# A convolution, attention and mixture-of-experts block on one core: the output buffer's wait moved from the store one tile back to the store two tiles back

## The chip, the core and the metric

The kernel runs on one core of a Trainium2 chip. The metric is the device time of one execution in microseconds (us), the median of several runs. The engines are named as the profile names them: PE (matrix products), DVE (vector), ACT (activation functions), POOL (GpSimd, which here issues all indirect DMAs) and SP (which issues plain DMAs).

## What is computed

The input is `x` of shape (4, 256, 32, 32). A convolution block with attention comes first, then multi-head attention over 4 x 1024 tokens of 256 channels, and then a mixture of eight experts, each a two-layer network with 1024 hidden units, of which every token goes to its best two. This last stage is the one that the change touches.

```python
logits = flat @ Wr
top_vals, top_idx = jax.lax.top_k(logits, TOP_K)          # TOP_K = 2
top_w = jax.nn.softmax(top_vals, axis=-1)
gates = zeros((N, E)).at[jnp.arange(N)[:, None], top_idx].add(top_w)
for e in range(E):
    hdn = jax.nn.gelu(flat @ W1[e] + b1[e], approximate=False)
    y = hdn @ W2[e] + b2[e]
    out = out + gates[:, e:e + 1] * y
t = t + out
```

## The kernel before

The 8192 pairs of token and expert are sorted by expert into lists in DRAM. The expert stage runs over 40 tiles of them: 31 wide ones of 256 places (`PAIRS`) and 9 narrow ones of 128 (`SINGLES`). A last step reads the result back, transposes it and stores the output. Each engine runs its own stream in program order, and the streams meet at semaphores. The order is written out by hand. For tile t:

- SP loads the tile's list (`load_list`, line 570). It waits until the store of tile t-6 has landed. Lists from tile 8 on are also held until every scatter of the last batch has landed (line 587) and the last batch's normalised rows are stored (line 494, one transfer of 1 MB, which waits for the last `tail_low` of DVE, line 2204).
- POOL gathers the tile's rows by that list (`gather`, line 772). In POOL's loop, iteration t first issues the gather of tile t+3, then, in the first five iterations, two to four scatters of the last batch's list entries (line 742), then it waits for the store of tile t-1 to land and counts `y_out` up (`output_landed`, line 788), and then it waits for `y_kept` and issues the store of tile t (`store_output`, line 782). That store is an indirect DMA that adds into `res1_d` in DRAM, two of them for a wide tile. Stores are so never in flight for two tiles at once.
- PE, in iteration t: first products of tile t (`first`, line 1023), transpose of the gathered rows of tile t+1 (`turn`, line 1407, which waits for the gather), second products of tile t-1 (`second`, line 1448, which ends with `y_made`). The result lies in one of two halves of a PSUM bank.
- ACT computes the hidden units of tile t (`gelus`, line 993).
- DVE, in iteration t: splits the hidden units of tile t+1 in two parts (`split_hidden`, lines 2015 and 2017) and, within that, copies the transposed rows of tile t+2 for PE (`keep_turned`, line 2003) and, for narrow tiles, that tile's first weights (`copy_first`, line 2226). In iterations 0 to 4 it then does some steps for the lists and the last `tail_low` steps. Last comes `keep_output` of tile t (lines 2026 to 2036): it waits for `y_made` and for `y_out`, writes the output buffer `ysb[t % 2]`, multiplies it by the gates, and counts `y_kept` up.

There are two output buffers, `ysb[0]` and `ysb[1]`, used in turn. `FREE` is 1, the value from which these semaphores start. The last tile, 39, is not stored by POOL. It is placed by matrix products of PE (`place_last`, line 1023 after the tiles) once DVE has split it (`halves_of_last`, lines 2054 and 2056). SP reads the result back once the store of tile 38 has landed (lines 600 and 605), PE transposes it (line 1506), DVE adds the last tile (line 2064), and SP stores it.

Of the kernel before, what the change touches and what calls it, by code (L numbers as in the profile page):

```python
# [82 lines left out]
FREE = 1  # L83
# [31 lines left out]
def hybrid_block(nc, x, wk, bk, wv, bv, wq, bq, wwg, bn1_g, bn1_b, bn1_m, bn1_v, wout, bout,  # L115
# [3 lines left out]
    def sem(name):  # L119
        return ctx.enter_context(nc.semaphore(name))  # L120
# [15 lines left out]
    with ctx:  # L136
# [166 lines left out]
        LAST = TILES - 1  # L303
# [51 lines left out]
        def s(name):  # L355
            if name not in S:
                S[name] = sem(name)
            return S[name]
# [1154 lines left out]
        def _(dve):  # L1513
# [506 lines left out]
            def gates(slot, a):  # L2020

                return list_of(slot)[:, a, 2:3].bitcast(F32)

            def keep_output(t, u, e, slot, wide=True):
                n = 2 if wide else 1
                dve.wait_ge(s("y_made"), FREE + t + 1)
                dve.wait_ge(s("y_out"), FREE + t - (t == LAST))
                dve.scalar_tensor_tensor(  # L2028
                    out=ysb[u][:, 0:n], in0=PP[2][:, u * HALF:u * HALF + n * C].rearrange("p (a c) -> p a c", a=n),
                    scalar=1.0 / WSCALE, in1=b2b[:, bass.ds(e, 1), :].broadcast_to((P, n, C)),  # L2030
                    op0=ALU.mult, op1=ALU.add)
                dve.drain()
                for a in range(n):
                    op = dve.tensor_scalar(ysb[u][:, a], ysb[u][:, a], gates(slot, a), None, ALU.mult)  # L2034
                if t < LAST:
                    op.then_inc(s("y_kept"), 1)
# [199 lines left out]
            for t in range(TILES):  # L2236
# [24 lines left out]
                if t in MARK_AT:  # L2261
                    mark_tokens(MARK_AT.index(t))
                keep_output(t, t % 2, e, t, t < PAIRS)
                if t == 0:
                    dve.wait_ge(s("cnt_made"), 1)
# [33 lines left out]
```

## Time and profile before

| | us |
|---|---|
| runs of the kernel | 1181.81 median (1177.8, 1181.81, 1184.69) |
| span of the profiled execution | 1183.2 |
| busy in it: PE / DVE / ACT / POOL | 1105.0 / 818.8 / 628.7 / 600.2 |

The span runs from the first to the last instruction of the profiled execution. The page gives no other time of that execution. Its span lies 1.4 us above the median of the runs and within what they show, so a difference that is worked out in the span is carried over to the median as it is.

### The profile page before, as it was taken

How to read it: one execution, taken by the hardware profiler on the slowest of the kernel's cores; microseconds unless marked ns; L12 is line 12 of the kernel's file. 1: busy time of each engine (PE TensorE's matmuls, PEld its weight loads, DVE VectorE, ACT ScalarE, POOL GpSimd, SP SyncE). 2: the span in 40 equal slices, each digit the busy share in tenths (PEclk: the TensorE clock that was granted, in tenths of full speed). 3: DMA queues.
4: the chain of work that ended last, by engine and by line, in shares of the span. 5: the costliest groups of instructions: out<-in, count | busy, mean ns of one | idle time of the engine just before them, and what ended most of it. 6: DMA issues, size and time to landing. Idle time of an engine off the chain costs nothing.

```text
span 1183.2 us, 28483 instructions
## 1 busy us (share of the span) xinstructions
PE 1105.0 (93%) x10344; PEld 728.7 (62%) x10344; DVE 818.8 (69%) x1493; ACT 628.7 (53%) x1144; POOL 600.2 (51%) x513
## 2 busy tenths in 40 slices
PE   7999999978999999999999989898999999999995
PEld 4454645434444454555445545687899988989883
DVE  4666566766788788788878892768555656655773
ACT  3566676546677666766775665453333333333332
POOL 3424242314888763775477546167545445544540
PEclk9999999989999999999999999999999999999999
DMA  5356842626123230433243213723333233323328
GB/s 173 89 181 211 311 160 94 184 69 196 51 56 87 82 82 29 104 100 98 68 115 91 60 43 100 303 38 77 53 54 54 43 52 55 46 46 47 46 38 289
DMA packets 98884, 120.60 MB, mean 102 GB/s; under 512 B 29024, under 2 KB 76064, under 8 KB 98112
## 3 DMA queue, kind: packets, MB, share of 16 engines
q1 hardware_dynamic: 75280, 70.40, 20.3%
q0 software_dynamic: 20400, 42.08, 15.9%
q10 hardware_dynamic: 3072, 6.30, 1.5%
q8 instruction: 89, 1.46, 0.5%
q14 instruction: 43, 0.35, 0.1%
HBM read 73.10 MB, written 45.47 MB: 100 GB/s over the span
## 4 chain that ended last, share of the span: by engine, by line
PE 70%; DVE 11%; issue 6%; DMA 6%; ACT 3%; DVEq 3%; POOL 1%; SPq 1%; ACTq 0%; POOLq 0%
PE PP L1023 21%; PE PP L1448 11%; PE PP L1307 9%; PE PP L1333 8%; PE PP L1122 3%; DVE mxp L1739 3%; PE PP L1254 3%; PE PP L1194 3%; PE PP L1039 3%; PE PP L1322 2%; PE PP L1317 2%; DMA res_d<-WORK,lb 2%; PE PP L1154 1%; DVEq L2016 1%; DVE WORK L2017 1%
## 5 line engine op out<-in xcount | busy, mean ns | idle before, releaser
L953 ACT ACTIVATE WB<-PP 128x512 f32<-128x512 f32 x512 | 268.6, 606 | 146.1 <-PE PP L1333 146.0
L1739 DVE TENSOR_REDUCE mxp<-PP 128x2 f32<-128x1024 f32 x242 | 287.0, 1219 | 62.3 <-PE PP L1254 62.0
L993 ACT ACTIVATE WORK<-PP,b1c 128x256 f32<-128x256 f32 (+1 forms) x320 | 139.4, 450 | 239.4 <-PE PP L1023 191.7
L699 POOL TENSOR_TENSOR WB<-WB 128x1024 f32<-128x1024 f32 x84 | 197.8, 2358 | 89.4 <-PE PP L1322 58.7
L782 POOL DMA_INDIRECT res_d<-WORK,lb x70 | 117.6, 1680 | 157.8 <-DVE WORK L2034 144.7
L1448 PE MATMUL PP<-WB,WORK 128*128 x1704 | 193.8, 274 | 0.0
L1023 PE MATMUL PP<-WORK,WB 128*128 128x256 f16 (+1 forms) x1552 | 175.9, 273 | 2.4 <-DVE WORK L2003 1.7
L1448 PEld LDWEIGHTS PP<-WB,WORK 128*128 128x128 f16 x1704 | 165.2, 98 | 19.6
L1023 PE MATMUL PP<-WORK 128*128 128x128 f16 (+6 forms) x1086 | 161.1, 300 | 11.3 <-DVE WORK L1656 3.6
L1023 PEld LDWEIGHTS PP<-WORK,WB 128*128 (+1 forms) x1552 | 152.2, 102 | 22.2 <-issue 4.8
L1333 PE MATMUL PP<-WORK 97*128 97x256 f16 x1024 | 158.0, 277 | 6.7 <-ACT WB L953 4.2
L666 POOL TENSOR_TENSOR WB<-WORK,WB 128x1024 f16<-128x1024 f32 x32 | 68.8, 2151 | 168.4 <-ACT WORK L841 168.3
L1023 PEld LDWEIGHTS PP<-WORK 128*128 128x128 f16 (+1 forms) x1086 | 100.5, 118 | 73.2 <-issue 22.6
L1307 PE MATMUL PP<-WB,WORK 128*32 128x256 f32 x2048 | 139.4, 390 | 2.9 <-ACT WB L939 1.6
L1333 PEld LDWEIGHTS PP<-WORK 97*128 97x128 f16 x1024 | 84.1, 98 | 80.2 <-ACT WB L953 46.1
L2017 DVE TENSOR_TENSOR WORK<-WORK 128x512 f16<-128x512 f32 (+1 forms) x160 | 101.6, 635 | 13.0 <-issue 1.3
L742 POOL DMA_INDIRECT list_d<-meta,idx x64 | 62.6, 978 | 59.3 <-issue 15.6
L2028 DVE SCALAR_TENSOR_TENSOR WORK<-PP,WORK 128x512 f32<-128x512 f32 (+1 forms) x40 | 25.2, 631 | 97.0 <-PE PP L1448 84.2
L772 POOL DMA_INDIRECT WORK<-rows_d,lb x70 | 71.7, 1025 | 37.9 <-issue 35.5
L1307 PEld LDWEIGHTS PP<-WB,WORK 128*32 128x32 f32 x2048 | 56.1, 110 | 52.6 <-issue 31.7
L2015 DVE CAST WORK<-WORK 128x512 f16<-128x512 f32 (+1 forms) x160 | 65.3, 408 | 21.1 <-ACT WORK L993 16.6
L1254 PE MATMUL PP<-WB 32*128 32x512 f16 x484 | 48.4, 387 | 10.9 <-DVE mxp L1739 5.9
(319 smaller groups left out, 1205.1 us busy)
## 6 DMA issues: line engine op xcount, KB each, us to landing
WORK<-in_L_ffn_W_dram POOLq DMA_DIRECT2D x32, 512.0 KB, 4.3
res_d<-WORK SPq DMA_DIRECT2D x8, 1024.0 KB, 5.2
late_d<-WB POOLq DMA_DIRECT2D x1, 6144.0 KB, 19.3
WB<-late_d ACTq DMA_DIRECT2D x3, 2048.0 KB, 14.0
v_d<-WORK SPq DMA_DIRECT2D x4, 1024.0 KB, 5.2
WORK<-q_hi_d SPq DMA_DIRECT2D x16, 256.0 KB, 3.7
WORK<-v_d SPq DMA_DIRECT2D x8, 512.0 KB, 5.6
WORK<-k_hi_d SPq DMA_DIRECT2D x16, 256.0 KB, 3.9
```

The lines of the kernel that those rows point to most:

```text
L699: pool.tensor_tensor(PS[n % 2], PR[n % 3][:, 0], PR[n % 3][:, 1], ALU.add).then_inc(s("pair_kept"), 1)
L772: pool.indirect_dma_start(xs[t % 2][:, a].rearrange("p s c -> p (s c)"), None, rows_d[0:(B if t >= EARLY else B - 1) * N, :], bass.Indirec ...
L782: pool.indirect_dma_start(res1_d[:, :], bass.IndirectOffsetOnAxis(ap=lb[:, t % LISTS, a, 1:2], axis=0), ysb[u][:, a], None, compute_op=ALU ...
L953: act.activation(PR[n % 3][:, c // 2, c % 2 * 2:c % 2 * 2 + 2], SCORES[m % 3] .rearrange("p (h n) -> p h n", h=2), ACT.Exp).then_inc(s("e_ ...
L993: act.activation(hid[:, k, 0:width], hidden_bank(k)[:, 0:width], ACT.Gelu, bias=b1c[:, bass.ds(e, 1), k], scale=1.0 / WSCALE)\
L1023: mm = pe.matmul(dst, lhsT, rhs, start=(n == 0), stop=(n == len(pairs) - 1))
L1254: mm = pe.matmul(PP[2 + h // 2][:, h % 2 * HALF:(h % 2 + 1) * HALF], QM[rows_at, g, at:at + P], KM[rows_at, g, k * HALF:(k + 1) * HALF], s ...
L1307: pe.matmul(WEIGHED[h * D:(h + 1) * D, 0:QN], VV[par][:, 2 * s4 + i, h * D:(h + 1) * D], PR[n % 3][:, i, h], start=(s4 + i == 0), stop=(s4 ...
L1333: mm = pe.matmul(SCORES[m % 3][:, i * QN:(i + 1) * QN], KP[g][0:QK_ROWS + 1, h, j * P:(j + 1) * P], QP[0:QK_ROWS + 1, g, h, q:q + QN], sta ...
L1448: mm = pe.matmul(PP[2][:, u * HALF + a * C:u * HALF + (a + 1) * C], lhsT, rhs, start=(n == 0), stop=(n == len(pairs) - 1))
L1739: dve.tensor_reduce(mxp[:, n // 4 % 2, i, h:h + 2, k], PP[2 + h // 2][:, :].rearrange("p (h n) -> p h n", h=2), X_AXIS, ALU.max).then_inc( ...
L2017: dve.tensor_tensor(hs[u][:, 1, k, 0:width], hid[:, k, 0:width], hs[u][:, 0, k, 0:width], ALU.subtract).then_inc(s("hs_kept"), 1)
```

## The change

DVE's `keep_output` waits on `y_out` before it writes the buffer. Before, it waited until the store of tile t-1 had landed, except for the last tile, where it was the store of tile t-2. Now it is the store of tile t-2 for every tile, the one that read the same buffer; tile 0 doesn't wait. Nothing else differs.

```diff
             def keep_output(t, u, e, slot, wide=True):
                 n = 2 if wide else 1
                 dve.wait_ge(s("y_made"), FREE + t + 1)
-                dve.wait_ge(s("y_out"), FREE + t - (t == LAST))
+                if t:
+                    dve.wait_ge(s("y_out"), FREE + t - 1)
                 dve.scalar_tensor_tensor(
```

## Rows read from the trace of the kernel before

**Rows 1.** The page: the span and the busy time of PE.
```profile
span 1183.2 us, 28483 instructions
PE 1105.0 (93%) x10344; PEld 728.7 (62%) x10344; DVE 818.8 (69%) x1493; ACT 628.7 (53%) x1144; POOL 600.2 (51%) x513
```
**Rows 2.** Waits from 760 us on: total us, times, longest us.
```profile
DVE WORK L2028 <- POOLq L788: 11.5, 6, 5.2
PE PP L1407 <- DMA WORK<-rows_d,lb: 5.9, 3, 3.1
```
**Rows 3.** Timeline of DVE, iterations 1 to 4: start us, us, [idle before <-releaser].
```profile
781.66 0.34 DVE L2100 TENSOR_REDUCE WORK<-WORK 128x23 f32<-128x184 f32 x1
787.25 0.69 DVE L2028 SCALAR_TENSOR_TENSOR WORK<-PP,WORK 128x512 f32<-128x512 f32 x1 [5.24 <-POOLq L788]
...
809.15 0.69 DVE L2028 SCALAR_TENSOR_TENSOR WORK<-PP,WORK 128x512 f32<-128x512 f32 x1 [0.26 <-issue]
...
815.95 0.69 DVE L2204 TENSOR_TENSOR WORK<-WORK 128x512 f16<-128x512 f32 x1
```
**Rows 4.** Timeline of PE, iterations 3 to 8.
```profile
787.53 0.62 PE L1407 MATMUL PP<-ident,WORK 128*128 128x128 f16 x8 [1.72 <-DMA WORK<-rows_d,lb]
...
815.32 5.41 PE L1023 MATMUL PP<-WORK,WB 128*128 128x256 f16 x48
823.79 1.04 PE L1407 MATMUL PP<-ident,WORK 128*128 128x128 f16 x8 [3.07 <-DMA WORK<-rows_d,lb]
...
836.04 0.61 PE L1407 MATMUL PP<-ident,WORK 128*128 128x128 f16 x8
...
846.97 0.61 PE L1407 MATMUL PP<-ident,WORK 128*128 128x128 f16 x8
```
**Rows 5.** Timeline of POOL in the same stretch.
```profile
779.28 1.63 POOL L782 DMA_INDIRECT res_d<-WORK,lb  x1 [0.30 <-issue]
...
784.42 0.97 POOL L772 DMA_INDIRECT WORK<-rows_d,lb  x1 [0.30 <-issue]
...
789.63 1.87 POOL L782 DMA_INDIRECT res_d<-WORK,lb  x1 [0.30 <-issue]
...
811.51 1.90 POOL L782 DMA_INDIRECT res_d<-WORK,lb  x1 [0.89 <-DVE WORK L2034]
...
817.22 1.05 POOL L772 DMA_INDIRECT WORK<-rows_d,lb  x1 [0.30 <-issue]
...
829.81 0.98 POOL L772 DMA_INDIRECT WORK<-rows_d,lb  x1 [0.30 <-issue]
```
**Rows 6.** Timeline of SP's DMA issues in the same stretch.
```profile
816.66 0.37 SPq L494 DMA_DIRECT2D rows_d<-WORK  x1
825.30 15.67 SPq L570 DMA_DIRECT2D lb<-list_d  x4
```
**Rows 7.** Windows: PE, PEld, DVE, ACT, POOL busy us (x), PEclk, DMA share, GB/s.
```profile
824.00:827.00 3.00, 3.00 (x22) 2.40 (x21) 2.85 (x6) 0.00 (x0) 2.70 (x2) 0.58 0.24 16
```
**Rows 8.** Timeline of DVE, narrow tiles.
```profile
1101.63 0.69 DVE L2028 SCALAR_TENSOR_TENSOR WORK<-PP,WORK 128x512 f32<-128x512 f32 x1 [1.59 <-POOLq L788]
...
1109.97 0.42 DVE L2028 SCALAR_TENSOR_TENSOR WORK<-PP,WORK 128x256 f32<-128x256 f32 x1 [2.24 <-POOLq L788]
...
1127.75 0.42 DVE L2028 SCALAR_TENSOR_TENSOR WORK<-PP,WORK 128x256 f32<-128x256 f32 x1 [0.32 <-POOLq L788]
...
1151.58 0.42 DVE L2028 SCALAR_TENSOR_TENSOR WORK<-PP,WORK 128x256 f32<-128x256 f32 x1 [1.75 <-POOLq L788]
```
**Rows 9.** Timeline of PE, narrow tiles.
```profile
1095.72 5.40 PE L1448 MATMUL PP<-WB,WORK 128*128 x48
...
1111.26 2.98 PE L1448 MATMUL PP<-WB,WORK 128*128 x24
...
1147.96 5.40 PE L1448 MATMUL PP<-WB,WORK 128*128 x48
```
**Rows 10.** The chain that ended last, in order of time: start us, us.
```profile
1147.46 3.85 DMA res_d<-WORK,lb
...
1153.21 3.85 DMA res_d<-WORK,lb
...
1157.12 3.89 DMA WORK<-res_d
```

## The prediction

> **What bounds the kernel now.** The page comes first: PE is busy for 1105.0 us of a span of 1183.2 us [rows 1]. So the change can only bring what PE, or the chain that ends the kernel, loses to the wait that it relaxes. The table of waits from 760 us on gives the ceiling: DVE stood before `keep_output` for the release by POOL 6 times, 11.5 us in all, 5.2 us at most [rows 2]. The same table shows the only wait of PE that DVE's lateness could reach in the wide tiles: 5.9 us for gathers, 3.1 us of it in one piece [rows 2]. The timelines then tell where these lie. One wait, 5.24 us, is at tile 1 [rows 3]. The other five are at the end: 1.59 us at tile 30, 2.24 at tile 31, 0.32 at tiles 34 and 36 (one row stands for both), 1.75 at tile 38 [rows 8]. In between, for tiles 2 to 29, the store one tile back has long landed and the change does nothing: PE runs from one transpose to the next in 10.93 us (846.97 - 836.04) [rows 4].
>
> **Tile 1 and what follows it.** DVE ended its table work at 782.00 and began the output of tile 1 at 787.25 [rows 3]. Now it begins at about 782.1, after PE's second products of that tile. The store itself gains nothing, since POOL is full with gathers and scatters without a gap other than 0.30 us and issues it at 789.63 [rows 5]. What moves is DVE's further work, but not by 5.2 us: the splits of tiles 3 to 5 wait for ACT and the copies of tiles 4 to 6 for PE's transposes, which stay where they are. Following these I find DVE about 4.1 us early at the output of tiles 2 and 3. Two things hang on that.
>
> First, POOL waited 0.89 us for DVE before the store of tile 3, where its ordinary gap is 0.30 [rows 5]. This 0.59 us is all that POOL gains, and the gather of tile 7, queued behind that store, starts its second half at 816.6 instead of 817.22 [rows 5].
>
> Second, the last `tail_low` of DVE starts about 3.9 us early (815.95 before [rows 3]), and so does SP's 1 MB store of rows, at 812.8 instead of 816.66 [rows 6]. Before, it was issued 0.56 us ahead of the second gather of tile 7, and that gather reached PE 6.57 us after its start (823.79 - 817.22) [rows 4, 5]. The gather of tile 4, with no such store beside it, took 3.11 us (787.53 - 784.42) [rows 4, 5]. I take that value now: the rows are 3.8 us further ahead, and the gather lands at 816.6 + 3.1 = 819.7. PE is free at 815.32 + 5.41 = 820.7, so its wait of 3.07 us at the transpose of tile 7 goes [rows 4]. With it goes a slower stretch: from this transpose to the next PE took 12.25 us where 10.93 is normal, 1.3 us more, and in that stretch the granted clock was 0.58, so in good part at the 1.2 GHz level, after the idle time [rows 4, 7]. Together PE could be 4.4 us early at the transpose of tile 8, at 831.65.
>
> What is late next is the gather of tile 8. Its list can't be loaded before the scatters have landed, which POOL issues right behind the gather of tile 7; SP's first such load was at 825.30 [rows 6]. They move by 0.6 us only. The second half of that gather started at 829.81 [rows 5]. With 3.1 us it landed at 832.9, and with the 0.6 us it lands at 832.3 to 832.7. PE then stands up to 1 us there and is early by 836.04 - 832.7 = 3.3 us. From tile 8 on nothing holds it and the gain stays. Bounds: 0 (the 1 MB store and the gather still meet) and 4.4 us. I take 3.2.
>
> **The narrow tiles.** Tile 30: PE ended its second products at 1095.72 + 5.40 = 1101.12 [rows 9], DVE started at 1101.63 [rows 8]; it now starts 0.16 us after PE, 0.35 us early. Tile 31: the wait of 2.24 us goes whole, and DVE is 2.24 + 0.24 (its start of tile 30 carried on, less the usual 0.1 us gap) = about 2.45 us early. Tile 32 is cut back by PE: its second products started at 1111.26 [rows 9], late through a gather that sits behind the store of tile 30 on POOL, and that moves by 0.35 us only. DVE so keeps about 1.95 us. The two waits of 0.32 us [rows 8] go as well: 1.95 + 0.64 = 2.6 us. In these tiles DVE has no other gap of size and PE follows its copies, so PE's last products, 1147.96 before [rows 9], are 2.6 us early too, and with them the last tile's placement.
>
> Tile 38, the store chain: before, its store was issued at 1153.21, which is 1.90 us after that of tile 37 had landed (1147.46 + 3.85 = 1151.31), landed at 1157.06, and the read back took 3.89 us [rows 10]. DVE's write and multiplication now lie beside the landing, so that 0.8 us of issue is left of the 1.90; with the 2.6 us this path is 3.4 to 3.7 us early. The end is set by the later of the two paths, PE's placement and the read back: 2.6 to 3.4 us. Bounds: 1.3 (PE alone sets the pace after tile 32) and 3.7. I take 2.7.
>
> **The sum.** 3.2 + 2.7 = 5.9 us, less 0.1 for POOL beside a busier DVE (below): 1183.2 - 5.8 = 1177.4 in the span, 1181.8 - 5.8 = 1176.0 as median. The removed wait of tile 0 costs nothing either way. The change adds no wait.
>
> **A price that speaks against it.** While DVE stood still, POOL's store of tile 0 took 1.63 us to issue; the next one, beside DVE's work, took 1.87 [rows 5]. Now DVE works from 783 to 787 us, where POOL issues five DMAs. At 0.24 us each that is up to 1.2 us on POOL; most of POOL's work of this stage already lies beside a busy DVE, so I take 0.1. The Trainium skill, SBUF — State Buffer, section "Who interferes with whom", says that DVE's two-port copies and casts lock GpSimd out of a shared pair of ports for the whole instruction, so that DMAs issued from it stall for want of descriptors. By that rule each of the five could be held for one instruction of DVE, 0.4 to 0.7 us in this timeline, 3.5 us at most, and the gain at tile 7 would be gone. The trace agrees in sign, with 0.24 us.
>
> **The rivals.** (a) Both gains come, 4.3 to 7.5 us: 1174.3 to 1177.5. Chance 0.50, a little under half of it beyond 5.9 us. (b) Only the end gains: the earlier 1 MB store and the two halves of the gather meet all the same, since store, gather and rows now share 813 to 820 us, and PE still waits at tile 7. 2 to 4 us, about 1179. For it: the same transfer made this gather slow before. Against it: 3.8 us of lead. Chance 0.22. (c) Only the beginning gains, because PE and DVE, nearly equally full in the narrow tiles, give each other new waits: 3 to 4.2 us, about 1178.5. Chance 0.09. (d) The wait is hidden anyway, or returns in full as POOL's own wait between stores, which still run one at a time: within 1.5 us of 1181.8. Against it: five waits lie at tiles where DVE itself sets the pace. Chance 0.07. (e) More than forecast: the gather of tile 8 doesn't hold PE and the end follows the store chain, 4.4 + 3.7 = 8.1 us, about 1173.5. Chance 0.08. (f) Slower: POOL's stream from 783 us to the gather of tile 7, six stores, six gathers and nine scatters, is lengthened by DVE's new timing by 0.25 us each, 5.2 us. Less the 0.6 us that POOL gains, PE's wait at tile 7 grows by 4.6 us. Against 2.7 us at the end this gives 1.9 us more, 1183.7. It decides from 0.6 + 2.7 = 3.3 us on. The same rule of the Trainium skill would bring it about. Chance 0.04.
>
> **How the numbers follow.** A measurement of this kernel can tell about 0.5%, 5.9 us, from no change, and the forecast of 5.8 us lies right at it. Beyond it lie nearly half of (a), all of (e), and a little of the rest through scatter of the runs: faster 0.40. Slower by so much only by scatter upon (f): 0.03. The rest, 0.57, is within. The range reaches from below (e) to past (d): 1171 to 1182. The likeliest case alone: 1174.3 to 1177.5.
>
> **What would show it.** In the profile after: no wait of DVE for POOL's release of any length; output of tile 1 at about 782 us; the 1 MB store near 813; PE's wait at the transpose of tile 7 gone or under 0.5 us, no fallen clock behind it, and a new wait of up to 1 us at tile 8; the transpose of tile 8 near 832.7; the output of tile 31 about 2.4 us sooner than the rest of the shift; the store of tile 38 about 0.8 us behind the landing of tile 37. The prediction is wrong if the wait at tile 7 is as long as before, or if POOL's gaps between 783 and 822 us grow.

## The result, and the profile of the changed kernel

| | before | changed |
|---|---|---|
| runs, median of 14 each | 1183.74 us (1177.8 to 1188.79) | 1176.21 us |
| ratio of the runs | | 0.9943, 95% interval 0.9925 to 0.9962 |
| span of the profiled execution | 1183.2 us | 1172.3 us |

One of the 14 runs of the changed kernel took 6132.73 us. The ratio leaves it out, and the others lie between 1173.04 and 1180.12, with a median of 1176.03. The ratio is 6.7 us of 1183.74, with an interval of 4.5 to 8.9 us. The two profiled executions are 10.9 us apart, more than the runs are. To see where this lies, both spans are cut at transposes and outputs that the timelines show. "Transpose of tile n" is PE's `turn(n)`, and "output of tile n" is DVE's first write of `keep_output`:

| stretch, us | before | changed | difference |
|---|---|---|---|
| start to transpose of tile 3 | 774.72 | 771.92 | -2.80 |
| to transpose of tile 8 | 61.32 | 55.87 | -5.45 |
| to transpose of tile 33 | 267.60 | 267.60 | 0 |
| to output of tile 39 | 49.89 | 47.69 | -2.20 |
| to the end | 29.67 | 29.22 | -0.45 |

The first row has no part of the change in it: up to there the two kernels wait for the same. The third is the same to 0.01 us, and it is so in all eleven further kernels below: from tile 8 to tile 33 PE sets the pace. All that the change does lies in the second row and the last two.

The page and the table of waits (from 740 us on) of the changed kernel answer to [rows 1, 2]. PE is busy for 4.6 us less, DVE's waits for POOL have shrunk from 11.5 us to one of 2.3, and PE's waits for gathers from 5.9 us to 2.5.

```profile
span 1172.3 us, 28483 instructions
PE 1100.4 (94%) x10344; PEld 728.6 (62%) x10344; DVE 818.2 (70%) x1493; ACT 629.0 (54%) x1144; POOL 598.8 (51%) x513
...
DVE WORK L2029 <- POOLq L788: 2.3, 1, 2.3
...
PE PP L1407 <- DMA WORK<-rows_d,lb: 2.5, 4, 1.3
```

The timeline of DVE in the changed kernel, beside [rows 3]. The output of tile 1 follows the table work at once. The last row is the output of tile 5, where the profile names POOL's count. It can't be that: the count which tile 5 needs is the landing of tile 3, and POOL had passed that before it issued the store of tile 4, at 816.90. It is a wait for PE, which ended tile 5's second products at 822.71 (817.31 + 5.40), 0.52 us before. In the kernel before this output starts 0.51 us after PE's end as well, and there the profile names PE.

```profile
778.76 0.34 DVE L2101 TENSOR_REDUCE WORK<-WORK 128x23 f32<-128x184 f32 x1
779.37 0.69 DVE L2029 SCALAR_TENSOR_TENSOR WORK<-PP,WORK 128x512 f32<-128x512 f32 x1 [0.26 <-issue]
...
800.90 0.69 DVE L2029 SCALAR_TENSOR_TENSOR WORK<-PP,WORK 128x512 f32<-128x512 f32 x1 [0.26 <-issue]
...
807.92 0.69 DVE L2205 TENSOR_TENSOR WORK<-WORK 128x512 f16<-128x512 f32 x1
...
823.23 0.69 DVE L2029 SCALAR_TENSOR_TENSOR WORK<-PP,WORK 128x512 f32<-128x512 f32 x1 [2.29 <-POOLq L788]
```

PE in the changed kernel, transposes of tiles 4, 7 and 8, beside [rows 4]. The waits of 1.72 and 3.07 us have become 0.69 and 0.20, and from tile 7 to tile 8 it takes 10.93 us instead of 12.25.

```profile
783.70 0.62 PE L1407 MATMUL PP<-ident,WORK 128*128 128x128 f16 x8 [0.69 <-DMA WORK<-rows_d,lb]
...
816.86 0.62 PE L1407 MATMUL PP<-ident,WORK 128*128 128x128 f16 x8 [0.20 <-DMA WORK<-rows_d,lb]
...
827.79 0.61 PE L1407 MATMUL PP<-ident,WORK 128*128 128x128 f16 x8
```

POOL in the changed kernel, beside [rows 5]: the third scatter of the last batch, first halves of the stores of tiles 1 and 3 with the second half of that of tile 2 between them, the second gather of tile 7, the gather of tile 8. The gather of tile 8 waits for its list, but not so that PE would notice.

```profile
772.50 0.96 POOL L742 DMA_INDIRECT list_d<-meta,idx  x1 [2.55 <-DMA list_d<-meta,idx]
...
785.29 1.62 POOL L782 DMA_INDIRECT res_d<-WORK,lb  x1 [0.30 <-issue]
...
797.63 2.11 POOL L782 DMA_INDIRECT res_d<-WORK,lb  x1 [0.31 <-issue]
...
806.65 1.62 POOL L782 DMA_INDIRECT res_d<-WORK,lb  x1 [0.30 <-issue]
...
811.78 0.98 POOL L772 DMA_INDIRECT WORK<-rows_d,lb  x1 [0.30 <-issue]
...
821.93 1.01 POOL L772 DMA_INDIRECT WORK<-rows_d,lb  x1 [1.50 <-DMA lb<-list_d]
```

The scatter in the first row waits for the two ahead of it to land. It comes 0.58 us after the transpose of tile 3 (771.92). In the kernel before it came 2.04 us after it (774.72):

```profile
776.76 0.96 POOL L742 DMA_INDIRECT list_d<-meta,idx  x1 [4.01 <-DMA list_d<-meta,idx]
```

Both lie ahead of the first output that the change can move, so this difference isn't the change's. The experiments come back to it.

SP in the changed kernel, beside [rows 6]: the row store is issued 3.15 us ahead of the second gather of tile 7. Before it was 0.56.

```profile
808.63 0.37 SPq L494 DMA_DIRECT2D rows_d<-WORK  x1
818.98 23.95 SPq L570 DMA_DIRECT2D lb<-list_d  x5
```

DVE at the end, outputs of tiles 30, 31, 32 and 38, beside [rows 8]. No output waits for a store any more. Three of these wait for PE instead.

```profile
1093.04 0.69 DVE L2029 SCALAR_TENSOR_TENSOR WORK<-PP,WORK 128x512 f32<-128x512 f32 x1 [1.25 <-PE PP L1448]
...
1099.05 0.42 DVE L2029 SCALAR_TENSOR_TENSOR WORK<-PP,WORK 128x256 f32<-128x256 f32 x1
...
1105.93 0.42 DVE L2029 SCALAR_TENSOR_TENSOR WORK<-PP,WORK 128x256 f32<-128x256 f32 x1 [0.95 <-PE PP L1448]
...
1140.47 0.43 DVE L2029 SCALAR_TENSOR_TENSOR WORK<-PP,WORK 128x256 f32<-128x256 f32 x1 [1.09 <-PE PP L1448]
```

What PE had of DVE's waits in the narrow tiles stands in the table of waits. The first row is the kernel before from 1103.6 us on (transpose of tile 33), the second the changed one from 1095.3 us on:

```profile
PE PP L1023 <- DVE WORK L2003: 2.7, 7, 0.8
```

```profile
PE PP L1023 <- DVE WORK L2003: 0.3, 1, 0.3
```

So before, PE waited seven times for DVE's copy of the transposed rows, and in the changed kernel it waits once: 2.4 us less. Of this, 0.5 us goes to longer waits for gathers (1.6 against 1.1 us).

### The profile page after: what moved, and what is told of

Same layout as the page of the kernel before. It is cut to its first block, busy times and chain, and to the rows that moved or that the text cites. A ratio compares the mean times of both kernels' runs of the same rounds, so it can differ in the third digit from the quotient of the medians.

```text
span 1172.3 us, 28483 instructions
## 1 busy us (share of the span) xinstructions
PE 1100.4 (94%) x10344; PEld 728.6 (62%) x10344; DVE 818.2 (70%) x1493; ACT 629.0 (54%) x1144; POOL 598.8 (51%) x513
## 4 chain that ended last, share of the span: by engine, by line
PE 74%; DVE 11%; issue 4%; DMA 4%; ACT 2%; DVEq 2%; SPq 1%; POOL 1%; ACTq 0%; POOLq 0%
PE PP L1023 22%; PE PP L1448 13%; PE PP L1307 9%; PE PP L1333 9%; PE PP L1194 4%; DVE mxp L1739 3%; PE PP L1122 3%; PE PP L1254 3%; PE PP L1039 3%; PE PP L1322 2%; PE PP L1317 2%; PE PP L1154 1%; DVE WORK L2017 1%; PE PP L1407 1%; DMA WORK<-rows_d,lb 1%
## 5 line engine op out<-in xcount | busy, mean ns | idle before, releaser
L1739 DVE TENSOR_REDUCE mxp<-PP 128x2 f32<-128x1024 f32 x242 | 287.0, 1219 | 60.7 <-PE PP L1254 60.4
```

Of the source, the lines that this page charges most:

```text
L1739: dve.tensor_reduce(mxp[:, n // 4 % 2, i, h:h + 2, k], PP[2 + h // 2][:, :].rearrange("p (h n) -> p h n", h=2), X_AXIS, ALU.max).then_inc( ...
```

## The experiments

The theory in hand: the change brings one gain early, through a gather that PE waits for at the transpose of tile 7, and one at the end, in the narrow tiles and the store of tile 38. The rival: the early one is scatter between executions. For every kernel the table at the end of this section gives the stretches. They come from one trace each; the times and ratios to the kernel before come from 9 to 12 runs. In some of these kernels the lines of the code are shifted by one to three.

**Tile 1 alone** (against the kernel before):

```diff
-                dve.wait_ge(s("y_out"), FREE + t - (t == LAST))
+                dve.wait_ge(s("y_out"), FREE + t - (t in (1, LAST)))
```

> Only tile 1's output is released from the wait on the store one tile back; tiles 2 to 38 wait as before. My theory: the whole early gain comes from this one wait, so the 1 MB row store is issued about 8 us ahead of the transpose of tile 7 instead of 7 us after the output of tile 3, PE's 3.07 us stand at the transpose of tile 7 falls under 0.5 us, and the time is 3 to 4.5 us below the kernel before. The narrow tiles show the five waits of before (1.6, 2.2, 0.3, 0.3, 1.8 us). Rival: the early part was scatter between executions (the trace after was already 2.8 us ahead before the expert stage's first output, and a landing of scatters took 1.5 us less), then this kernel is within 1 us of before and PE still waits 2 us or more at the transpose of tile 7.

Measured: 1182.09 us, ratio 0.9977 (0.9958 to 0.9996), 2.7 us. DVE's timeline shows why it is no more: tile 1 goes at once, and tile 2 waits 3.49 us for the store of tile 1. By tile 3 DVE is within 0.5 us of its old time, counted from the transpose of tile 4 (21.15 against 21.62 us).

```profile
783.69 0.69 DVE L2028 SCALAR_TENSOR_TENSOR WORK<-PP,WORK 128x512 f32<-128x512 f32 x1 [0.26 <-issue]
...
797.34 0.69 DVE L2028 SCALAR_TENSOR_TENSOR WORK<-PP,WORK 128x512 f32<-128x512 f32 x1 [3.49 <-POOLq L788]
...
809.04 0.69 DVE L2028 SCALAR_TENSOR_TENSOR WORK<-PP,WORK 128x512 f32<-128x512 f32 x1 [0.26 <-issue]
```

The row store is issued at 816.54, again 0.56 us ahead of the second gather of tile 7 (817.10), and PE waits 1.48 us. My theory that one wait carries the early gain falls: the wait passes on.

**Tiles 1 and 2**: the same edit with `t in (1, 2, LAST)`.

> Tiles 1 and 2 released from the wait on the store one tile back, the others as before. With tile 1 alone released, tile 2 waited 3.5 us in its place. Theory: with both released DVE is as early as in the changed kernel from the output of tile 2 on, the row store is issued about 3 us ahead of the second gather of tile 7, that gather takes about 5 us, and PE waits under 0.6 us at the transpose of tile 7; the time is 2 to 4 us below before and 0.5 to 1.5 us below the kernel with tile 1 alone. Rival: the wait passes on to tile 3 (2 us or more) and the time is that of the kernel with tile 1 alone.

Measured: 1181.9 us, ratio 0.9969 (0.9944 to 0.9993), 3.7 us by the ratio, with an interval of 0.8 to 6.6, and so the time of the kernel with tile 1 alone. The rival had it: now tile 3 waits.

```profile
796.29 0.69 DVE L2028 SCALAR_TENSOR_TENSOR WORK<-PP,WORK 128x512 f32<-128x512 f32 x1 [0.31 <-PE PP L1448]
...
810.03 0.69 DVE L2028 SCALAR_TENSOR_TENSOR WORK<-PP,WORK 128x512 f32<-128x512 f32 x1 [2.93 <-POOLq L788]
```

**Tiles 30 to 38 alone**: the same line with `t >= 30`.

> Only tiles 30 to 38 are released from the wait on the store one tile back; tiles 1 to 29 wait as before. My theory: 2.2 to 2.7 us below the kernel before, all of it after the transpose of tile 33; tile 1 shows its wait of about 5 us and the transpose of tile 7 its wait of about 3 us. Rival (the gain at the end is a by-product of the earlier start of the whole stage): nothing, within 1 us of before.

Measured: 1178.2 us, ratio 0.9952 (0.9928 to 0.9976), 5.7 us with an interval of 2.8 to 8.5. In the trace the last tile's output comes 46.91 us after the transpose of tile 33, 2.98 us sooner than before, and the end 0.58 us sooner after that, 3.6 us in all. The rest of the 5.7 has no place in this trace that the edit could reach. The early stretch is a finding of its own. With the old wait untouched there, tile 1 waits 1.99 us and tile 2 0.66, and PE waits 1.07 us at the transpose of tile 7: 56.69 us from tile 3 to tile 8, where the profile of before took 61.32. So I expected the waits of before and they were less than half. The early loss differs between executions of the same code. And by the runs this kernel, with nothing changed early, is within the noise of the changed one (0.9952 against 0.9943): these two don't show an early gain.

**The row store held, in the changed kernel:**

```diff
+            sp.wait_ge(s("y_made"), FREE + 5)
             store_rows(B - 1, B)
```

> The changed kernel, in which SP in addition holds the 1 MB row store of the last batch until PE has finished the products of tile 4, so that it is issued within 1 us of the second gather of tile 7, as it was before. DVE is as early as in the changed kernel. Theory A (the store and the gather met, my prediction): PE waits 2.5 to 3.5 us at the transpose of tile 7 again, the clock falls behind it, and the time is 3 to 4.5 us above the changed kernel, that is 2 to 3.5 us below the kernel before. Theory B (what counts is that POOL issues the gather 0.6 us earlier): PE waits under 1 us there and the time is that of the changed kernel within 1 us.

Measured: 1178.11 us, ratio to before 0.9954 (0.993 to 0.9978), 1.9 us above the changed kernel by the medians, though the two intervals overlap. SP issued the store at 815.35, 0.66 us ahead of the second gather, and PE:

```profile
822.53 0.62 PE L1408 MATMUL PP<-ident,WORK 128*128 128x128 f16 x8 [1.97 <-DMA WORK<-rows_d,lb]
...
833.47 0.61 PE L1408 MATMUL PP<-ident,WORK 128*128 128x128 f16 x8
```

The gather took 6.52 us (822.53 - 816.01), as against 5.08 in the changed kernel (816.86 - 811.78) and 6.57 before. So the meeting cost 1.4 us here, less than half of the 3.5 that I took it for. No clock fell behind this wait: it is 10.94 us to the next transpose, at a granted clock of 1.00. The size is no constant, though. This is the second gather of tile 7 in the traces that keep POOL's order, from its issue to the transpose of tile 7:

| row store issued ahead of it by | us |
|---|---|
| 0.56 (before; tile 1; scatters held in before; tile 38) | 6.57, 5.30, 5.79, 6.12 |
| 0.66 (changed, row store held) | 6.52 |
| 1.85 (tiles 1 and 2; tiles 30 to 38; 30 and 31) | 5.09, 6.02, 6.02 |
| 3.15 (changed) | 5.08 |
| 3.27 (changed, scatters held) | at most 4.40, PE doesn't wait |
| behind it (next experiment) | at most 4.04, PE doesn't wait |

The five at 0.66 us or less all lie above those at 3.15 and 3.27, but they differ by 1.3 us among themselves. The closest pair is this kernel and the changed one with the scatters held (below): their third scatters come 1.90 and 2.03 us after the transpose of tile 3, DVE is equally early, and the early stretch takes 58.37 and 56.27 us.

**The row store moved behind the gather, in the kernel before:**

```diff
+            sp.wait_ge(s("ld_xs1"), rows_loaded(7))
             store_rows(B - 1, B)
```

> The kernel before, with DVE's wait as it was, in which SP holds the 1 MB row store until the gather of tile 7 has landed. DVE and POOL are as late as before. Theory A (store and gather met): the second gather of tile 7 takes 3 to 3.5 us instead of 6.6, PE's wait at the transpose of tile 7 is under 0.5 us; the list of tile 8 is then late in its place, so that PE waits at the transpose of tile 8, 3 to 6 us, and the time is between 2 us below and 2 us above before. Theory B (the gather is late because POOL issues it late): PE waits 2.5 us or more at the transpose of tile 7 as before.

Measured: 1182.76 us, ratio 0.9985 (0.9964 to 1.0006). PE doesn't wait at tile 7 and waits at tile 8 instead, as expected, though less:

```profile
824.09 0.61 PE L1408 MATMUL PP<-ident,WORK 128*128 128x128 f16 x8
...
837.06 0.62 PE L1408 MATMUL PP<-ident,WORK 128*128 128x128 f16 x8 [1.88 <-DMA WORK<-rows_d,lb]
```

The second gather was issued at 820.05, so it took at most 4.04 us with no row store beside it.

**Why the early loss differs.** Put side by side, the traces with the old wait at tiles 1 to 29 and nothing else changed early differ in one thing. POOL's third scatter of the last batch waits for the first two to land. It came 0.08 and 0.29 us after the transpose of tile 3 in two of them (tiles 30 to 38; tiles 30 and 31), with 56.7 us to tile 8, and 2.04 and 1.80 us after it in two others (before; tile 38), with 61.3 and 60.7. DVE's wait at tile 1 was 1.99 and 1.89 us in the first two, 5.24 and 4.38 in the others. Of the nine traces with the gathers in their old places and no hold, five have the early landing (0.08 to 0.58 us) and four the late one (1.80 to 2.10); the change isn't what decides it, for both kinds occur with and without it. So I held the scatter, in both kernels, until DVE has split the third part of the hidden units of tile 2, 2.03 us after the transpose of tile 3 in either trace:

```diff
                         pool.wait_ge(s("st_list"), 16 * (2 * NT * (B - 1) + 2))
+                        pool.wait_ge(s("hs_kept"), FREE + 11)
```

> The kernel before, in which POOL holds the third scatter of the last batch until DVE has split the sixth hidden chunk of tile 2, that is until about 2.0 us after the transpose of tile 3, where the traces show 0.1 to 0.6 us in some executions and 1.8 to 2.1 us in others. Theory (the size of the early wait is set by when these scatters land, which varies between executions): DVE's wait at tile 1 is 4.3 to 5.3 us, PE waits 2.4 to 3.1 us at the transpose of tile 7, and from the transpose of tile 3 to that of tile 8 it takes 60.5 to 61.5 us; the time is 1 to 3 us above the kernel before. Rival: the row store alone decides it, and that stretch takes 56.7 us in spite of the hold.

> The changed kernel with the same hold. Theory: DVE no longer waits for the store, the row store is issued 2 us or more ahead of the second gather of tile 7, PE waits 1.4 to 1.7 us at the transpose of tile 4 and under 0.6 us at that of tile 7; from the transpose of tile 3 to that of tile 8 it takes 56.8 to 57.3 us, 4 us less than the kernel before with the hold, against 0.8 us where the scatters landed early. Rival: the late scatters delay POOL so that PE waits at tile 7 whatever DVE does, and the stretch takes 59 us or more.

Measured: the kernel before with the hold 1185.85 us, ratio 1.0014 (0.9989 to 1.0039); the changed one with it 1178.88 us, 0.9951 (0.9926 to 0.9976). The medians are 7.0 us apart and the intervals don't overlap. The outputs of tile 1, before and changed, both with the hold:

```profile
788.81 0.69 DVE L2029 SCALAR_TENSOR_TENSOR WORK<-PP,WORK 128x512 f32<-128x512 f32 x1 [4.65 <-POOLq L788]
```

```profile
786.89 0.69 DVE L2030 SCALAR_TENSOR_TENSOR WORK<-PP,WORK 128x512 f32<-128x512 f32 x1 [0.26 <-issue]
```

The hold brought DVE's long wait back as expected, but PE waited 1.88 us at tile 7, and the stretch took 58.86 us, less than the 60.5 that I expected. So the landing of the scatters accounts for DVE's wait and for part of PE's. The changed kernel took 56.27 with it, less than 56.8. The change is worth 2.6 us there, not 4. With it the row store is issued 3.27 us ahead of the second gather of tile 7, and PE doesn't wait for that gather:

```profile
820.29 0.98 POOL L772 DMA_INDIRECT WORK<-rows_d,lb  x1 [0.30 <-issue]
```

```profile
824.69 0.62 PE L1408 MATMUL PP<-ident,WORK 128*128 128x128 f16 x8
```

What makes the difference to the 61.3 and 60.7: in those two PE waited 3.07 and 2.57 us at tile 7, and the next transpose came 12.25 and 12.60 us later instead of 10.93. Behind waits of 1.88 and 1.97 us it came after 10.94. The transpose of tile 7 itself came 47.92 us after that of tile 3 with the hold, and 48.05 with tile 38 alone. So between these two nearly all of the difference is the slower stretch behind the wait.

**Tiles 30 and 31 alone**: `t in (30, 31, LAST)`.

> Tiles 30 and 31 alone released. Theory: the output of tile 31 comes 2.4 to 2.7 us sooner after the transpose of tile 33 than before (9.0 us before), the waits of 0.3 us at later tiles and that of 1.7 us at tile 38 stay, and the last tile's output comes 1.7 to 2.2 us sooner after the transpose of tile 33 than before (49.9 us before). Rival: PE and DVE are nearly equally full there, so that half of it or more is lost by the last tile: 1 us or less.

Measured: 1180.44 us, ratio 0.9971 (0.9947 to 0.9996). The output of tile 31 comes 3.66 us after the transpose of tile 33 (1104.78 - 1101.12), where before it came 6.33 us after it (not 9.0, as the expectation has it), so it is 2.67 us sooner. At the last tile 0.87 us is left of it (49.02 against 49.89). The rival had the size and named the wrong cause. It is not PE's pace. Tile 32 now waits for the store of tile 31:

```profile
1104.78 0.42 DVE L2028 SCALAR_TENSOR_TENSOR WORK<-PP,WORK 128x256 f32<-128x256 f32 x1
1112.17 0.42 DVE L2028 SCALAR_TENSOR_TENSOR WORK<-PP,WORK 128x256 f32<-128x256 f32 x1 [1.47 <-POOLq L788]
```

**Tile 38 alone**: `t >= 38`.

> Tile 38 alone released. Theory: its store is issued about 1 us sooner, but the last tile's products and PE's placement of it are not, and the end goes by the later of the two: its output comes at the same 49.9 us after the transpose of tile 33, and from there to the end nothing over 0.3 us is gained. Rival: the read back of the result alone sets the end, then the end comes about 1 us sooner.

Measured: 1182.29 us, ratio 0.9984 (0.9957 to 1.0011). The last tile's output comes 50.32 us after the transpose of tile 33, not sooner than before. From there to the end it takes 29.19 us. The six traces with the old wait at tile 38 and the gathers in their old places have 29.37 to 30.06, mean 29.83. By this stretch about 0.6 us is gained, more than the 0.3 of my theory and less than the rival's 1 us. The chain that ended last runs through PE's placement of the last tile here, and through the read back in the kernel before [rows 10]. But the runs show no gain, and the two stretches together, 79.51 us, are those of before (79.56) and of the row store behind the gather (79.53). So this one trace doesn't show that releasing tile 38 brings anything by itself.

**Each gather one tile sooner**, in the changed kernel:

```diff
-            for t in range(3):
+            for t in range(4):
                 gather(t)
             for t in range(TILES):
-                if t + 3 < TILES:
-                    gather(t + 3)
+                if t == 5:
+                    gather(8)
+                if t != 4 and t + 4 < TILES:
+                    gather(t + 4)
```

> The changed kernel, in which POOL issues each gather one tile sooner (ahead of the store of the tile before it; the gather of tile 8 stays where it was). Theory: what PE still waits for in the expert stage is gathers queued behind stores and scatters on POOL, 0.7 to 1.7 us at the transpose of tile 4, 0.2 us at tile 7, 1.3 us at tile 34, 0.3 us at tile 37. With the gathers ahead these waits fall under 0.3 us each, whether the row store meets a gather or not, and the time is 2 to 3.5 us below the changed kernel, about 0.992 of the kernel before. Rival: PE's and DVE's own pace takes the place of these waits, or the stores come later on POOL for the gathers ahead of them, and the gain is under 1 us.

Measured: 1174.64 us, ratio 0.9916 (0.9886 to 0.9946). PE waits for no gather any more in the stage; the transposes of tiles 4, 7, 8 and 34:

```profile
784.26 0.61 PE L1409 MATMUL PP<-ident,WORK 128*128 128x128 f16 x8
...
817.04 0.61 PE L1409 MATMUL PP<-ident,WORK 128*128 128x128 f16 x8
827.97 0.61 PE L1409 MATMUL PP<-ident,WORK 128*128 128x128 f16 x8
...
1101.36 0.39 PE L1409 MATMUL PP<-ident,WORK 128*128 128x128 f16 x4
```

By the stretches it is 1.2 us shorter to tile 8, 1.5 us shorter to the last output, and 0.5 us longer at the end than the changed kernel: 2.3 us. By the ratios it is 3.2 us, but their intervals overlap, so the runs don't show it to be faster than the changed kernel. It has the lowest median and the shortest span of the study.

**The same in the kernel before**, with its old wait:

> The kernel before, with its wait on the store one tile back, in which POOL issues each gather one tile sooner. Theory: the early loss is a late gather, not DVE's wait itself, so the stretch from the transpose of tile 3 to that of tile 8 takes 54.6 to 55 us as with both changes, with DVE's wait of 2 to 5 us still at tile 1; at the end the waits of 1.6, 2.2, 0.3 and 1.7 us stay and the last tile's output comes 49 to 50.3 us after the transpose of tile 33. The time is 2 to 5 us below before. Rival: DVE's lateness reaches PE by another way (the copies of the transposed rows), and the stretch takes 56 us or more.

Measured: 1182.64 us, ratio 0.9988 (0.9963 to 1.0012). The early stretch took 55.44 us, a little over what I expected, with DVE's waits of 1.97 and 1.05 us still at tiles 1 and 2. DVE's lateness there costs PE 0.8 us (55.44 against 54.64) once the gather isn't late. At the end it is worse than before, 52.18 us to the last output against 49.89. DVE waits 2.40 us for the store at tile 31, and the wait at tile 36 has grown to 1.65 us, where it was 0.32. Why it grew wasn't tried; a gather is now queued ahead of each landing, so that POOL's count may come later. Here the rival of the expectation holds: behind both waits PE stood for DVE's copy of the transposed rows, 2.43 and 2.17 us. The products behind the first took 4.29 us instead of 2.85, with a granted clock of 0.50 from 1106.2 to 1108.5 us.

```profile
1101.16 0.42 DVE L2030 SCALAR_TENSOR_TENSOR WORK<-PP,WORK 128x256 f32<-128x256 f32 x1 [2.40 <-POOLq L788]
...
1132.99 0.42 DVE L2030 SCALAR_TENSOR_TENSOR WORK<-PP,WORK 128x256 f32<-128x256 f32 x1 [1.65 <-POOLq L788]
```

```profile
1106.25 4.29 PE L1025 MATMUL PP<-WORK 128*128 128x128 f16 x48 [2.43 <-DVE WORK L2005]
...
1138.58 2.85 PE L1025 MATMUL PP<-WORK 128*128 128x128 f16 x48 [2.17 <-DVE WORK L2005]
```

The stretches of all kernels, in us, each from one trace:

| kernel | to tile 3 | tile 3 to 8 | tile 33 to output 39 | output 39 to end |
|---|---|---|---|---|
| before | 774.72 | 61.32 | 49.89 | 29.67 |
| changed | 771.92 | 55.87 | 47.69 | 29.22 |
| tile 1 alone | 776.32 | 57.02 | 49.97 | 29.99 |
| tiles 1 and 2 | 777.49 | 57.73 | 50.48 | 30.00 |
| tiles 30 to 38 | 774.51 | 56.69 | 46.91 | 29.09 |
| changed, row store held | 775.10 | 58.37 | 47.18 | 29.15 |
| before, row store behind the gather | 779.91 | 57.15 | 50.16 | 29.37 |
| before, scatters held | 776.87 | 58.86 | 50.21 | 30.06 |
| changed, scatters held | 779.35 | 56.27 | 47.64 | 29.24 |
| tiles 30 and 31 | 776.80 | 56.72 | 49.02 | 29.86 |
| tile 38 | 778.64 | 60.65 | 50.32 | 29.19 |
| changed, gathers sooner | 773.33 | 54.64 | 46.14 | 29.69 |
| before, gathers sooner | 771.60 | 55.44 | 52.18 | 29.77 |

## Why the prediction was right, and where its steps were not

Forecast was 1176.0 us, 5.8 us less than before; the runs give 1176.21 us and 6.7 us (4.5 to 8.9). That the two times agree to 0.2 us is luck: the forecast started from 1181.81 us for the kernel before, and its 14 runs gave 1183.74. The difference is what was forecast, and there the forecast is 0.9 us short. It was to come a little over half from the early stretch (3.2 us) and the rest from the end (2.7 us). By the traces the end brings 3.4 us and the early stretch 0.8, 2.6 or 4 to 5 us, as the scatters land and the clock falls. The sums, about 4 to 8 us, cover what the runs show.

The early part has no measurement of its own in the runs: tiles 30 to 38 alone gave 5.7 us (2.8 to 8.5), so that against the rival "only the end gains" speak the traces and the experiments on the row store and the gathers, and not the runs. The two kernels with the scatters held come nearest, with medians 7.0 us apart.

The steps of the forecast did less well than its sum.

**The end: right, undersized.** Six traces with the old wait up to tile 37 need 50.17 us on average to the last output (before, tile 1, tiles 1 and 2, row store behind the gather, scatters held, tile 38), and four with the new wait 47.36: 2.8 us. The four traces without the old wait lie at 46.91 to 47.69, the six with it at 49.89 to 50.48. From the last output to the end it takes 29.83 on average in the six traces with the old wait at tile 38 against 29.18 in the five without (the two kernels with gathers sooner are left out), 0.65 us more. Added up, 3.45 us where I took 2.7. For the pair of before and changed alone it is 2.65 (2.20 + 0.45).

The 2.6 us for PE was about right. What I missed is how close the two paths are: the chain that ended last runs through the read back in the traces of before and changed, and through PE's placement in those of tiles 30 to 38 and of tile 38 alone. In all thirteen traces the end comes 29.8 to 30.4 us after the issue of the store of tile 38. In the changed kernel this store is issued 46.71 us after the transpose of tile 33 instead of 49.57, 2.9 us early and not 3.4 to 3.7. It comes 1.2 us behind the landing of tile 37, where I forecast 0.8, since the output of tile 38 now waits for PE (1.09 us).

Tile by tile it went as worked out: tile 31 2.67 us early against the transpose of tile 33 (2.45 forecast), tile 32 1.66 (1.95), cut back by PE's wait for the gather of tile 34, 1.30 us.

**The early stretch: right in kind, and the size is not one number.** I took 3.2 us. The profiles differ by 5.45, of which 1.03 us is PE's shorter wait at the transpose of tile 4 (0.69 against 1.72 us). That comes ahead of anything that DVE does differently, so it isn't the change's. The other 4.4 is what I had as my upper bound. But the kernels with the old wait took 56.7 to 61.3 us for this stretch, the changed one 55.87, and 56.27 with the scatters held. So the change is worth 0.8 us where the scatters land soon, 2.6 with them held, and 4 to 5 where PE's wait reaches 2.6 us and the slow stretch of PE follows. Each of these is a difference of single traces. I read a single execution's wait of 5.24 us as the kernel's. It was a late one.

**Two steps failed inside it.** First, the gather was to take 3.1 us, as with no row store beside it: it took 5.08 even though the row store was issued 3.15 us ahead, where I worked out 3.8. It is 5.3 to 6.6 us when they meet and at most 4.0 with no row store. Moving it brought 1.5 us between these two traces, not 3.5. Second, "0.59 us is all that POOL gains": from the second gather of tile 4 to that of tile 7 POOL took 31.61 us (811.78 - 780.17) instead of 32.80 (817.22 - 784.42), 1.19 us less. The wait of 0.89 us before the store of tile 3 went, as forecast, and its DMAs were issued faster. Together with the gather of tile 4, which took 3.53 us (783.70 - 780.17) where it took 3.11 before, this makes up for 1.0 of the 2.0 us that the gather of tile 7 took longer than forecast. The other 1.0 us is what it was to land ahead of PE. So PE's wait is 0.20 us, near the 0 of the forecast, by luck in part.

**The gather of tile 8** was to hold PE for up to 1 us. It didn't: POOL issued its second half at 823.25 and PE came at 827.79. My error was again POOL, which was further ahead than I had it.

**That the change does nothing for tiles 2 to 29 was wrong**, though the sum didn't rest on it. The wait is absent there in the trace of before because DVE was late already. With tile 1 released it stood at tile 2 (3.49 us), with tiles 1 and 2 at tile 3 (2.93 us), and with tile 31 at tile 32 (1.47 us). In five of the kernels with the old wait there, tile 5 waited for POOL too, 2.3 to 3.4 us, and it cost PE nothing from there on: from tile 8 to tile 33 they take the same 267.60 us. So a release at one tile is worth little, because the next tile takes the wait over, and a wait counts only where it reaches PE, here through a late gather or a late copy.

**The price that speaks against it** rested on a misread row. I took the 1.63 us of the store of tile 0, from 779.28 us on [rows 5], as those of a POOL beside a standing DVE. DVE stood from 782.00 to 787.25; beside that store it was at its table work:

```profile
779.86 0.51 DVE L2089 TENSOR_SCALAR WORK<-WORK 128x40 f32<-128x40 f32 x1
```

So the 0.24 us isn't what a busy DVE costs, and "the trace agrees in sign" doesn't stand. The price didn't fall due as a whole: POOL's store of tile 1 took 1.62 us to issue in the changed kernel, where it took 1.87 before, but it took 1.62 as well in two traces with the old wait (scatters held; tile 38). The first half of that of tile 3 took 1.62 against 1.90. POOL's stretch got shorter though DVE stood less. By the prediction's estimate from the rule of the Trainium skill (SBUF — State Buffer, "Who interferes with whom") it would have been longer, by up to 3.5 us, so the rule doesn't decide here. It isn't refuted either: the second half of the store of tile 2 took 2.11 us, in the changed kernel. What lengthens a single one of these wasn't isolated.

**The clock.** Behind PE's waits of 3.07 and 2.57 us the next transpose came 1.3 and 1.7 us late, with a granted clock of 0.58 over the 3 us behind the first [rows 7] and 0.63 behind the second. Behind 1.88 and 1.97 us it came on time, with a granted clock of 1.00. In the narrow tiles of the kernel before with the gathers sooner, a wait of 2.43 us has a granted clock of 0.50 behind it, and the products behind one of 2.17 us took their usual 2.85. That the wait causes it is what the order of events suggests. It wasn't tried by itself.

Left open: why the scatters land about 1.6 us sooner in some executions, why the same gather with the row store 0.56 us ahead of it takes 5.3 us in one and 6.6 in another, and why the part up to the transpose of tile 3 takes 771.9 to 779.9 us in the eleven kernels with the gathers in their old places, whose code is the same up to there. That is more than the change is worth.

## What to carry to other kernels

A wait that is one step too strict shows in a trace only at the step where it is the last to be met; released there alone it passes on to the next step, so look at the whole chain of steps before pricing it, and release all of them. Before pricing a stall from one profile, find what sets its length: here a landing of DMAs that differs by about 1.6 us between executions went with a stall of about 2 us or of 4 to 5 us. Compare two executions by stretches cut at the same instructions, since the stretches that the change can't reach (here 2.8 of 10.9 us) would otherwise be counted as its gain.

## What was not expected of the hardware

An indirect gather of 128 rows took 5.3 to 6.6 us from issue to use with a plain 1 MB store issued 0.6 us ahead of it (five traces), 5.1 to 6.0 with it 1.85 us ahead (three), 5.1 and at most 4.4 with it 3.2 us ahead (two), and 4.0 at most with none ahead of it (one). The issue of an indirect store of 128 rows took POOL between 1.6 and 2.1 us in either kernel, and a busier DVE beside it didn't make the whole row of them slower.
